# GpSimd makes the plain lane one-hots of the edge sort

## What is computed

```python
x = x + gnn(layernorm(x), ..., edge_index=stack([src, dst]))   # eight heads of 64, then one output layer
x = x + moe(layernorm(x), ...)                                 # 8 experts, the best two of each node
# in each layer of gnn:
score = s_src[src] + s_dst[dst]
e = exp(-leaky_relu(score, 0.2))
h_prime = segment_sum(e[:, None] * h[dst], src, num_segments=6250)
```

## Time and profile before

| | |
|---|---|
| median of three runs | 6812.87 us |
| profiled execution | 6819.92 us, span 6818.2 us |
| TensorE busy (matmul) | 76% of the span |
| VectorE busy | 63% |
| ScalarE busy | 35% |
| GpSimd busy | 48% |
| mean granted TensorE clock | 0.892 |
| the sweep, first to last by_lane product | about 562 to 1429 us |

### The profile page before, as it was taken

One profiled execution on the slowest core, in us unless ns is written; L12 is line 12 of the kernel. 1 busy time (PEld: TensorE's weight loads), 2 busy tenths in 40 slices (PEclk: granted clock), 3 DMA queues, 4 the chain that ended last, 5 costly groups with the idle time before them and its releaser, 6 DMA issues. The chain is left out here.

```text
span 6818.2 us, 96747 instructions
## 1 busy us (share of the span) xinstructions
PE 5204.5 (76%) x21312; PEld 2869.0 (42%) x21312; DVE 4268.2 (63%) x15762; ACT 2400.1 (35%) x6496; POOL 3282.8 (48%) x3459
## 2 busy tenths in 40 slices
PE   4577888867777777877777775787787787787777
PEld 2222222233333333333333333565565565565555
DVE  4688999976777776767667673444444444444443
ACT  2005777732333333333333332233333333333333
POOL 0000000006666666666666664666666666666662
PEclk8789999988999989989999997788888888888998
DMA  2100000007777676767677775444444444444444
GB/s 81 48 1 0 0 0 0 0 14 202 204 201 203 200 204 194 202 199 202 197 202 202 201 193 135 115 119 114 118 116 115 118 117 116 118 119 113 119 116 52
DMA packets 325651, 847.60 MB, mean 124 GB/s; under 512 B 73909, under 2 KB 97661, under 8 KB 325256
## 3 DMA queue, kind: packets, MB, share of 16 engines
q0 software_dynamic: 224256, 690.38, 37.9%
q1 hardware_dynamic: 101000, 152.57, 7.4%
HBM read 816.28 MB, written 26.36 MB: 124 GB/s over the span
## 5 line engine op out<-in xcount | busy, mean ns | idle before, releaser
L988 POOL DMA_INDIRECT heads_rows<-table,shared_node_of x1712 | 1624.9, 949 | 992.5 <-issue 454.2
L988 POOL DMA_INDIRECT out_rows<-table,shared_node_of x1712 | 1636.7, 956 | 967.5 <-issue 440.5
L1174 PE MATMUL heads_banks<-heads_rows,heads_hot 128*128 128x512 f32 x3424 | 1863.0, 672 | 313.4 <-DVE heads_rows L1045 180.1
L1174 PE MATMUL out_banks<-out_rows,out_hot 128*128 128x256 f32 x3424 | 1263.2, 461 | 281.2 <-issue 152.4
L1045 DVE TENSOR_TENSOR heads_rows<-heads_rows,heads_ps_k 128x512 f32<-128x512 f32 x1712 | 1160.8, 678 | 4.2 <-DVE heads_ps_k L1080 3.3
L1121 ACT ACTIVATE sums<-heads_banks x856 | 510.7, 599 | 1771.9 <-PE heads_banks L1174 1050.6
L1174 PEld LDWEIGHTS heads_banks<-heads_rows,heads_hot 128*128 128x128 f32 x3424 | 626.8, 206 | 859.5 <-issue 740.1
L1121 ACT ACTIVATE late_sums<-out_banks x856 | 327.0, 384 | 1747.6 <-PE out_banks L1174 1076.5
L1174 PEld LDWEIGHTS out_banks<-out_rows,out_hot 128*128 128x128 f32 x3424 | 663.0, 219 | 477.8 <-issue 319.4
L853 PE MATMUL sort_ps_a<-sort_by_tile,sort_by_lane 125*128 125x367 f16 x1650 | 542.1, 330 | 148.0 <-ACT sort_by_lane L766 84.1
L496 POOL IOTA sort_member<- 1x856 f32 x1 | 4.8, 4767 | 1233.6 <-PE sort_ps_b L883 1233.6
(11 more groups left out here) (345 smaller groups left out, 6560.3 us busy)
## 6 DMA issues: line engine op xcount, KB each, us to landing
heads_lanes<-lane_rows SPq DMA_DIRECT2D x214, 256.0 KB
out_lanes<-lane_rows SPq DMA_DIRECT2D x214, 256.0 KB
heads_rows<-table,shared_node_of POOLq DMA_INDIRECT x1712
out_rows<-table,shared_node_of POOLq DMA_INDIRECT x1712
table<-proj_rows SPq DMA_DIRECT2D x50, 253.9 KB
table<-mid_rows SPq DMA_DIRECT2D x50, 127.0 KB
proj_x_raw<-in_x POOLq DMA_DIRECT2D x5, 1250.0 KB, 15.5
moe_x_raw<-in_x SPq DMA_DIRECT2D x50, 125.0 KB
```

Of the source, the lines that this page charges most:

```text
L988: nc.gpsimd.indirect_dma_start(out=rows[:, g % RING, j, :], out_offset=None, in_=table[:, :], in_offset=bass.IndirectOffsetOnAxis(ap=node_ ...
L1174: ins = nc.tensor.matmul(banks[:, bass.ds(info[r], width)], hot[:, g % HOTS, j, :], rows[:, g % RING, j, 0:width], start=False, stop=True, ...
```

## The change

GpSimd gets one instruction for each column of slots 1, 3 and 4, 990 in all, written out one after the other without a loop. Each waits for its own value of `slot_used`. VectorE no longer makes `plain_lane`; a new semaphore, `lane_known`, tells GpSimd that `lane` of the part is there. Two unused semaphore names are dropped.

```diff
+            for part in range(PARTS):
+                pool.wait_ge(s["lane_known"], part + 1)
+                for n in range(PCOLS):
+                    if n % SLOTS in SCALED:
+                        pool.wait_ge(s["slot_used"], part * PCOLS + n + 1)
+                        nc.gpsimd.tensor_scalar(plain_lane[:, SCALED.index(n % SLOTS), :], lanes_h[:, :], lane[:, n:n + 1], None,
+                                                ALU.is_equal).then_inc(s["lane_made"], 1)
             pool.wait_ge(s["route_used"], PARTS * TB)
...
-                seq.mark(nc.vector.tensor_copy(lane[:, :], scratch_i[:, 0:PCOLS]))
+                nc.vector.tensor_copy(lane[:, :], scratch_i[:, 0:PCOLS]).then_inc(s["lane_known"], 1)
                 seq.mark(nc.vector.tensor_copy(tile[:, :], place_i[:, :]))
+                dve.wait_ge(s["lane_known"], part + 1)
                 seq.wait()
...
                         dve.wait_ge(s["slot_used"], n + part * PCOLS + 1)
-                        if slot in SCALED:
-                            nc.vector.tensor_scalar(plain_lane[:, SCALED.index(slot), :], lanes_h[:, :], lane[:, at], None,
-                                                    ALU.is_equal).then_inc(s["lane_made"], 1)
-                        else:
+                        if slot not in SCALED:
```

More of the change, by code:

```diff
@@ L445, in sort_edges @@
                  "numbered lane_made scaled slot_made slot_used swept high_out packed_made packed_turned turn_out reach_made step_made "
-                 "step_known route_made route_used block_known row_cleared cast held held_pe held_act is_keyed is_spread is_compared ranks_out picked "
+                 "step_known route_made route_used block_known row_cleared cast held_act lane_known is_keyed is_spread is_compared ranks_out picked "
                  "local_made local_turned lane_kept lanes_stored")
```

## The result

The change makes the kernel 0.8% faster: 6768.82 us (median of six runs, 6758.31 to 6774.44) against 6818.66 (six runs of the kernel before beside them, 6806.22 to 6841.54). The ratio is 0.9919, its 95% interval 0.9899 to 0.994. I had forecast +59 us; it is -50.

The account below looks back on a forecast made before the run. VectorE was taken to bound the sweep at 2.50 us a turn; less 0.48 removed, plus 0.66 lost to GpSimd, gave 2.68. Over 330 turns that is +59 us, a median of 6872 us, range 6700 to 7010.

Parts of the forecast that it names:

- What bounds the kernel, and what is removed: Sweep: VectorE sets the 2.50 us turn; removing three L640 at 0.16 us gives 2.02, 158 us over 330 turns.
- VectorE's loss for each GpSimd one-hot: Sweep: each GpSimd one-hot costs VectorE 0.22 us (bounds 0 and 0.37), three 0.66 us a turn.
- the sum: Sweep turn: 2.50 - 0.48 + 0.66 = 2.68 us, so +59 us over 330 turns.
- the sign turns at 0.16: Sweep: the change gains or loses according to whether VectorE's loss per GpSimd one-hot is under or over 0.16 us.
- GpSimd's own instruction: Sweep: GpSimd's one-hot takes 0.3 to 0.4 us, about 1 us a turn, so its own throughput doesn't bind.
- The ring: Sweep, one-hot to freed slot with GpSimd: 1.9 us for five columns, under 2.02; floor 2.05 to 2.2 us a turn.
- the free port: Rival, sweep: port free most of the time; c = 0.10 gives 6753 us, c = 0 gives 6665 to 6714; chance 0.32.
- c = 0.10: Free-port example, sweep: VectorE loses 0.10 us per GpSimd one-hot; turn 2.32 us, time 6753 us.
- Full exclusion: Rival, sweep: VectorE loses 0.37 us per GpSimd one-hot; turn 3.13 us, time 7021 us; chance 0.14.
- GpSimd isn't starved: Rival, sweep: GpSimd too late, slow (6929 us) or without a turn beside back-to-back VectorE instructions (7077 us); chance 0.09.

Follow-up runs that it names:

- the floor run: Changed kernel with no one-hots from GpSimd, ScalarE multiplying zeros and waiting for the slot itself: ratio to the kernel before 0.9757, sweep 711.7 us.
- Beside the kernel before: Kernel before, nothing taken from VectorE, plus 990 GpSimd one-hots that nothing reads: ratio 1.0134, turn 2.80 us, sweep 967.6 us.
- the tight ring: Changed kernel, but GpSimd waits for one more TensorE column than it needs (four columns for plain one-hots): ratio 1.0118, sweep 950.5 us.
- the deep ring: Changed kernel with 15 plain buffers instead of 3; GpSimd waits for ScalarE alone, ScalarE for the slot: ratio 0.9838, sweep 772.8 us.
- The two-a-turn runs: Changed kernel with slots 1 and 4 on GpSimd, slot 3 on VectorE: ratio 0.9989; the same with 15 plain buffers, GpSimd running ahead: 1.0017.

## Why the prediction was wrong

*What bounds the kernel, and what is removed.* Right. VectorE sets the turn of 2.50 us, three L640 are worth 0.16 each, and without them the turn is 2.02 (the floor run: 2.018, 160.8 us). TensorE and ScalarE keep up.

*VectorE's loss for each GpSimd one-hot: the step that failed.* I took 0.22 us, between 0 and 0.37, from the AFFINE_SELECT's 0.28 and the belief that by_tile would lose all of it. In the changed kernel the longer distances between VectorE's own instruction starts add up to some 80 us over the sweep, 0.08 each; with the ring's part it is 0.106, so that three cost 0.32 us a turn where the sum had 0.66. Beside the kernel before it is 0.096 each. That GpSimd slows VectorE was right and the size was not: the sign turns at 0.16, as the prediction says, and the measured value lies on the other side. The rows that I had were both true, an L1049 that lost nothing and an L1013 that lost all of 0.12, and the sweep too has instructions that lose nothing and others that lose 0.13. My mistake was to take the loss as most of the length of GpSimd's instruction. That length is twice what I took (0.60), and VectorE loses a sixth of it or less.

The prediction cites the Trainium skill ("SBUF — State Buffer", "Who interferes with whom"): whichever of the two engines issues first keeps the shared ports for its whole instruction. The runs agree that the two engines get in each other's way, but not that VectorE is shut out for GpSimd's whole instruction: then three of 0.60 us would add 1.8 us to a turn of the kernel before (an estimate), and they add 0.30. The rule is for VectorE instructions in a two-port mode; the rows do not show in which mode these run.

*GpSimd's own instruction.* I took 0.3 to 0.4 us, nearest to AFFINE_SELECT; it is 0.597 at the least and 0.695 in the mean. A row with another operation of the same width was a poor price. The cost did not show as GpSimd being full (0.7 x 3 = 2.1 us of 2.34), but in the ring.

*The ring.* I summed 1.9 us, "0.1 us to spare", with 0.28 for GpSimd. With 0.60 the same sum is 2.24, and the tight ring measures 2.19. So the ring comes up to where VectorE stands, and VectorE now and then finds no free slot. The account of the changed kernel's sweep closes so: 711.7 + some 80 (delays) + some 25 (what is left, of which some 18 is VectorE idle before L648 and L652, beyond its idle time before) = 817 us. Taking GpSimd out of TensorE's ring gives back 40 to 44 us. In the deep ring about half of that is VectorE's idle time (22 us less), and the delays also fall, from some 80 to some 67 us: the ring and the delays are not independent of each other.

*The rivals.* The one that came true is the free port, the one with the other sign; its example of c = 0.10 gave 59 us less than before, measured are 50 less. That it comes so near is partly luck. Its 0.10 was the difference between two AFFINE_SELECTs (0.28 less 0.18). By the same reasoning GpSimd's tensor_scalar, 0.60 less 0.27, would cost 0.33 us each. Full exclusion is ruled out, and GpSimd isn't starved: beside back-to-back VectorE instructions it took 0.78 us (median) instead of 0.60.

*What stays open.* Why one GpSimd one-hot costs 0.06 us in one arrangement and 0.18 in another. The losses come in steps of about 0.03, 0.06 to 0.09 and 0.13 us on single VectorE instructions, and where the turns are steady they repeat the same meetings each time; with two a turn most losses are those of 0.13. Which part of which instruction they meet in, the trace doesn't show. The two-a-turn runs also show that a loss measured in one pattern doesn't foretell that of another.

## What to carry to other kernels

Moving some of a full engine's instructions (3 of 12 a turn here) to an idle one pays by what they cost from start to start (0.16 us here, not the record's 0.25), less what the helper's instructions cost the full engine. A first estimate of that second number can be had by itself: let the helper run them unread beside the unchanged kernel. Here that gave 0.096 us each, and the changed kernel lost 0.106; but it would not have told the 0.15 and 0.18 of the versions with two a turn. Then look at which event frees the helper's buffer. Here it waited for the last reader's follower, TensorE, when its own reader ScalarE had been done for some 0.5 us (763.92 to 764.46 in the earlier trace rows); a wait on ScalarE's count with the same three buffers takes the sweep from 817 to 777 us, and that version (ratio 0.984 on its chip, with 15 buffers 0.9838 on another) beats both kernels. Handing over only some of the instructions is no safe middle way: two of three gained nothing that could be measured, one of three 0.2%.

## What the hardware showed unexpectedly

A GpSimd tensor_scalar over 125 x 128 takes 0.53 us at the least with a constant (add or compare, fp16 or fp32) and 0.60 with a number for each partition, about double an AFFINE_SELECT of this width (0.28). What it costs VectorE's 16-bit instructions beside it is far less than its length and differs by form and by where the two meet: in the mean 0.001 us for 2 columns, 0.015 for a memset, 0.03 for 128 columns with a constant, 0.10 with a number for each partition, and up to 0.18 for the same instruction in another arrangement. A record that grows need not cost pace: beside a gather instruction in the earlier trace rows one VectorE record went from 0.33 to 0.53 us with no delay behind it.
